# Output projection halves together, second norm one slot earlier, head scales between two expert products

## The chip, the cores and the metric

The kernel runs on one core of one Trainium2 chip. The metric is the device time of one execution in microseconds, the median of several runs. It is a single program written out for each engine: PE (TensorE), ACT (ScalarE), DVE (VectorE), POOL (GpSimd) and SP (SyncE), which issues the DMAs.

## What is computed

A transformer layer on tokens of shape 16 x 256 x 128 in fp32: 16 sequences of 256 tokens, width 128. All inputs beside the tokens are weights.

```python
x = L0_attn_tokens
x = x + attn(layernorm(x))       # 16 heads, keys of 16, values of 64
x = x + moe(layernorm(x))        # 16 experts of width 64, top 4, and a shared expert

# attn: q, k, v l2-normed per head
sim = einsum('bhid,bhjd->bhij', q, k)
aggr = einsum('bhij,bhjd->bhid', square(relu(sim)), v)
out = tanh_norm(aggr) * tanh(silu(gates))      # tanh_norm scales each head's row
return out @ Wout

# moe: scores = sigmoid(x @ gate_kernel) + bias; 2 best of 4 groups, then 4 best experts
y = sum over the experts of combine * (silu(x @ w_gate) * (x @ w_up)) @ w_down
return y + (silu(x @ sw_gate) * (x @ sw_up)) @ sw_down
```

## The kernel before

**Steps and stages.** The kernel works on one sequence of 256 tokens at a time and overlaps seven stages of different sequences. `step(s)` runs for s = -2 to 18. In step s the attention proper (A) is done for sequence s, the first norm and the q/k and v products (L) for s + 2, the gate products and norms of values (P, N) for s + 1, the attention output and the second norm (O) for s - 1, the experts (F) for s - 2 and the expert output (D) for s - 3. `OFFSET` holds these distances. In steps 2 to 13 every stage runs.

**Slots.** A step has eight slots, one for each pair of heads. `FILL` (lines 44 to 54) is an order written out by hand: for each slot the jobs that PE does between the attention products. In a slot PE does the jobs of `FILL[k]`, then the scores of pair k + 1 (line 467), then the values product of pair k (line 499). The values product waits for POOL, which squares the relus (line 326, two multiplies of 128 x 512 in each slot). The relus themselves are ACT's (line 601, two in each slot, ahead of all else that ACT does in it).

**The jobs that matter here.** `qk` and `v`: products of the normed tokens (lines 358 to 360, three matmuls of a high and low split each). `gu` 0 to 8: gate and up products of a pair of experts, the last that of the shared expert. `rT` and `cT`: transposes of the head scales and of the routing weights (line 411). `rB` and `cB` 0 to 3: their spreading over the partitions (line 417). `y` 0 and 1: the two token halves of the attention output projection (line 421), which wait until all four `rB` are read. `x2T`: transposes of the second norm's rows (line 426), `lg`: router logits (line 430), `y2` 0 and 1: the expert output (line 440), which waits until all four `cB` are read.

**Banks.** The fillers share four PSUM banks. The job with number n in `ORDER` (the fill order run together, skips included) has bank n modulo 4, and `wait_for_bank` makes it wait until the job four places before it has been read (the `read` semaphores); where that one is a skip or does not run, the next four before. `evacuate` (ACT) follows the same fill order: it copies `xT`, `qk`, `v`, `x2T`, `rT`, `cT` out of PSUM and does the silu of `gu`. DVE's reads are written by hand in its own `step`.

**The other engines around the change.** DVE's list has for each slot: `gated_heads` (line 901, needs ACT's square of the pair, line 610), `gate_up` (line 855: up times silu, frees the bank of `gu`), `scale_heads` and `scale_hidden` (lines 863 and 872, free `rB` and `cB`), `low_parts` (line 737, frees `qk`), `sums` (line 744, from ACT's squares of `v`), `residual_row` (line 911, frees `y`), `row_stats` (lines 670 to 675), `normed_rows` (line 679, releases `x2T`). `head_scales` waits for ACT's tanh of the norms (line 618, behind the silu of product 4) and then has four short instructions on 128 x 32 elements, each waiting for the one before or queued behind it: lines 783, 788, 789 and 790; the last releases `rT`. POOL has in each slot the two multiplies of line 326, in slots 4 to 7 also one of the values' scaling (line 344), in slot 1 the root of the first norm, in slot 6 that of the second (`root`, line 317). The root waits for `row_stats`. SP's list has the load of the residual rows (waits for `y`), the load of the tokens, the store of the q/k rows (waits for both `low_parts`) and their loads in another layout.

Of the kernel before, what the change touches and what calls it, by code (L numbers as in the profile page):

```python
# [12 lines left out]
P = 128  # L13
# [8 lines left out]
def bass_attn_moe_layer_kernel(nc, tokens, Wqg, Wkv, Wout, gate_kernel, gate_bias,  # L22
# [20 lines left out]
    SKIP = ("-", "skip", 0)  # L43
# [8 lines left out]
        [("L", "qk", 1), ("L", "v", 0), ("F", "cB", 1), ("L", "v", 1), SKIP],  # L52
        [("L", "v", 2), ("F", "cB", 2), ("L", "v", 3), ("F", "cB", 3), ("O", "x2T", 0), SKIP],
    ]
    ORDER = [job for slot in FILL for job in slot]
    assert len(FILL) == SLOTS and len(ORDER) % 4 == 0
# [8 lines left out]
    FIRST_STEP, LAST_STEP = -2, B + 2  # L65

    with ExitStack() as ctx:
# [213 lines left out]
        def _(pool):  # L281
# [37 lines left out]
            def step(s, q, on, at):  # L319
                for k in range(SLOTS):  # L320
                    if "A" in on:
                        for h in (2 * k, 2 * k + 1):

                            wait(pool, values_done, 8 * s + (h - 4) // 2 + 1)
                            pool.wait_ge(relu_done, 16 * s + h + 1)
                            pool.tensor_tensor(p[h % 4][:], r[h % 2][:], r[h % 2][:], ALU.mult).then_inc(probs_done, 1)  # L326
                    if k == 1 and "L" in on:
                        pool.wait_ge(ch_l, 3 * (s + 3))
                        root(rstd1, var1, rstd1_ready)
                    if k == 1 and at == FIRST_STEP:  # L330
                        tables()
                    if k == 6 and "O" in on:
                        pool.wait_ge(ch_n, 3 * s)
                        root(rstd2, var2, rstd2_ready)
                    if "P" in on:
                        b = s + 1
                        if k in (4, 5, 6, 7):

                            t, half = divmod(k - 4, 2)
                            pool.wait_ge(vs_ready, b + 1)  # L340
                            pool.wait_ge(read["v"], 4 * b + k - 3)
                            view = v[b % 3][:, t, half * 512:(half + 1) * 512].rearrange("p (h d) -> p h d", d=DV)
                            scale = vs[:, t, half * NP:(half + 1) * NP]
                            pool.tensor_tensor(view, view, broadcast(scale, [P, NP, DV], 2), ALU.mult)\  # L344
                                .then_inc(v_normed, 1)

            run_flat(step)

# [283 lines left out]
        def _(dve):  # L633
# [209 lines left out]
            def step(s, q, on, at):  # L843
# [70 lines left out]
                for k in range(SLOTS):  # L914
# [23 lines left out]
                    if k == 2:  # L938
# [5 lines left out]
                            gate_up([2])  # L944
                        gated_heads(k)
                        if F:
                            gate_up([3, 4])
                    if k == 3:
                        if O:
                            head_scales(link_o, b)  # L950
                            link_o.end()
                        gated_heads(k)
                        if F:
                            gate_up([5])
# [27 lines left out]
                    if k == 5:  # L982
# [4 lines left out]
                        if O:  # L987
                            dve.wait_ge(x_back[pq], (b - pq) * 8 + 16)
                            residual_row(0)
                        if L_on:  # L990
                            low_parts(0, s + 2)
                        if O:
                            residual_row(1)
                            dve.wait_ge(read["y"], 2 * b + 2)
                            row_stats(link_n, x1[pq], st2, mv2, var2)
                            link_n.end()
                        if F:
                            scale_hidden([0])
                    if k == 6:
                        gated_heads(k)  # L1000
                        if L_on:
                            low_parts(1, s + 2)
                        if at == FIRST_STEP:
                            value_weights()
                        if L_on:
                            sums(0, s + 2)
                        if F:
                            scale_hidden([1])
                        if O:
                            wait(dve, done["lg"], b)  # L1010
                            dve.wait_ge(rstd2_ready, b + 1)
                            normed_rows(x1[pq], mv2, rstd2, xn2, ln2_ready)
                        if L_on:
                            sums(1, s + 2)
                    if k == 7:
                        gated_heads(k)
                        if L_on:
                            sums(2, s + 2)
                        if F:
                            scale_hidden([2])  # L1020
                        if L_on:
                            sums(3, s + 2)
                        if F:
                            scale_hidden([3])
                        if O:
                            dve.wait_ge(x2h_ready, b + 1)
                            dve.tensor_tensor(x2l[:], bank[("x2T", 0)][:, 0:N], x2h[:].bitcast(F32), ALU.subtract)\
                               .then_inc(read["x2T"], 1)

            run_flat(step)  # L1030

# [20 lines left out]
```

## Time and profile before

| what | value |
|---|---|
| median of 3 runs | 753.18 us (752.52 to 755.59) |
| the profiled execution | 755.62 us |
| its span, first to last instruction | 753.6 us |
| PE busy | 680.0 us, 90% of the span |
| PE weight loads | 525.0 us, 70% |
| DVE busy | 543.5 us, 72% |
| ACT busy | 431.8 us, 57% |
| POOL busy | 354.3 us, 47% |
| mean granted clock of TensorE | 0.971 |
| chain that ended last | PE 48%, DVE 29%, ACT 12%, issue 9% |

The profile is that of one execution. Its busy times are sums over the whole span, with a start in which the stages fill up and an end in which they run dry. In a timeline each row is a group of equal instructions: its start, how long from the first's start to the last's end, engine, line, operation, what it writes and reads, how many; in brackets the idle time of that engine before it and what ended it. The granted clock is given as a share of full speed.

### The profile page before, as it was taken

What the parts mean: (1) busy time and instruction counts of PE and PEld (TensorE: products, weight loads), DVE (VectorE), ACT (ScalarE), POOL (GpSimd) and SP (SyncE); (2) the same over time, 40 slices, a digit from 0 to 9 for tenths busy, and PEclk for the clock granted to TensorE, in tenths of its full rate; (3) what the DMA queues carried; (4) which work ended last, traced back from release to release, by engine and by line L of the source; (5) the groups of instructions that cost most, each with busy time, mean ns of one, the idle gap of its engine ahead of it and who ended that gap; (6) DMA issues with size and microseconds to landing.
All of it is one profiled execution on the core that took longest, in us unless ns stands there. A gap on an engine that the chain in (4) does not pass through costs nothing.

```text
span 753.6 us, 15281 instructions
## 1 busy us (share of the span) xinstructions
PE 680.0 (90%) x5160; PEld 525.0 (70%) x5160; DVE 543.5 (72%) x1739; ACT 431.8 (57%) x986; POOL 354.3 (47%) x368
## 2 busy tenths in 40 slices
PE   3676898999999999999999999999999999998876
PEld 2544476777777777777777777777777777666775
DVE  4555558687887968687877968686878868686653
ACT  4575666656665675656666675756566656453211
POOL 3245565554646464554555463645546464643000
PEclk9887999999999999999999999999999999999789
DMA  9994949394654829191845739190927548000000
GB/s 265 112 142 58 137 57 127 39 139 52 119 72 93 97 69 113 31 141 29 131 59 106 85 79 106 64 117 18 152 33 118 66 91 92 2 15 2 8 7 8
DMA packets 72829, 61.24 MB, mean 81 GB/s; under 512 B 8624, under 2 KB 72496, under 8 KB 72752
## 3 DMA queue, kind: packets, MB, share of 16 engines
q1 hardware_dynamic: 72752, 60.26, 54.8%
q8 instruction: 42, 0.69, 0.4%
q14 instruction: 35, 0.29, 0.1%
HBM read 41.37 MB, written 18.87 MB: 80 GB/s over the span
## 4 chain that ended last, share of the span: by engine, by line
PE 48%; DVE 29%; ACT 12%; issue 9%; DMA 1%; POOL 1%; DVEq 0%; SPq 0%; ACTq 0%; POOLq 0%
PE ps_f L440 9%; PE ps_f L421 8%; PE ps_a L499 7%; PE ps_f L358 6%; PE ps_f L360 4%; PE ps_f L359 4%; DVE it L855 4%; DVE norms_y L663 3%; ACT sq L565 3%; DVE norms_t L662 3%; PE ps_s L467 3%; PE ps_f L400 3%; ACT v L562 2%; ACT r L601 2%; DVE it L872 2%
## 5 line engine op out<-in xcount | busy, mean ns | idle before, releaser
L326 POOL TENSOR_TENSOR p<-r 128x512 f32<-128x512 f32 x256 | 263.8, 1051 | 316.0 <-ACT r L601 283.2
L601 ACT ACTIVATE r<-ps_s 128x512 f32<-128x512 f32 x256 | 141.8, 618 | 84.0 <-PE ps_s L467 79.7
L499 PE MATMUL ps_a<-p,v 128*64 128x256 f32 x1024 | 146.2, 397 | 3.0 <-DVE big L901 1.6
L499 PEld LDWEIGHTS ps_a<-p,v 128*64 128x64 f32 x1024 | 64.5, 137 | 43.3 <-POOL p L326 4.8
L593 ACT ACTIVATE it<-ps_f 128x256 f32<-128x256 f32 x144 | 55.5, 385 | 64.4 <-PE ps_f L360 61.3
L901 DVE TENSOR_TENSOR big<-ps_a,wt 128x256 f32<-128x256 f32 x128 | 53.6, 420 | 39.6 <-ACT big L610 38.5
L855 DVE TENSOR_TENSOR it<-ps_f,it 128x256 f32<-128x256 f32 x144 | 58.9, 419 | 29.4 <-ACT it L593 28.8
L440 PE MATMUL ps_f<-wdown,it 128*128 128x128 f32 x576 | 71.3, 285 | 3.3 <-DVE it L872 3.3
L440 PEld LDWEIGHTS ps_f<-wdown,it 128*128 128x128 f32 x576 | 68.7, 199 | 4.3 <-DVE it L872 4.3
L467 PE MATMUL ps_s<-qkt 64*128 64x256 f32 x512 | 66.0, 333 | 3.4 <-ACT r L601 1.9
L344 POOL TENSOR_TENSOR v<-v,vs 128x512 f32<-128x512 f32 x64 | 66.6, 1042 | 3.4 <-DVE vs L778 3.4
L610 ACT ACTIVATE big<-ps_a 128x256 f32<-128x256 f32 x128 | 53.3, 416 | 25.9 <-PE ps_f L400 23.4
L421 PEld LDWEIGHTS ps_f<-wout,big 128*128 128x128 f32 x512 | 61.5, 197 | 5.8 <-issue 5.8
L421 PE MATMUL ps_f<-wout,big 128*128 128x128 f32 x512 | 65.3, 283 | 0.0
L467 PEld LDWEIGHTS ps_s<-qkt 64*128 64x128 f32 x512 | 39.1, 186 | 26.6 <-issue 11.4
L744 DVE TENSOR_REDUCE norms_m<-sq 128x8 f32<-128x512 f32 x64 | 43.7, 683 | 19.1 <-ACT sq L565 19.1
L571 ACT ACTIVATE wt<-ps_f 128x512 f32<-128x512 f32 x64 | 38.4, 600 | 29.4 <-PE ps_f L360 28.9
L737 DVE TENSOR_TENSOR qk_parts<-ps_f,qk_parts 128x512 fp32r<-128x512 f32 x32 | 22.1, 691 | 42.5 <-ACT qk_sq L557 42.5
L358 PE MATMUL ps_f<-x2h,weg_hi 128*128 128x256 f32 x144 | 48.6, 337 | 4.0 <-DVE it L855 2.6
L562 ACT ACTIVATE v<-ps_f 128x512 f32<-128x512 f32 x64 | 41.9, 654 | 6.6 <-PE ps_f L360 4.0
L863 DVE TENSOR_TENSOR big<-ps_f,big 128x512 f32<-128x512 f32 x64 | 42.2, 684 | 4.7 <-PE ps_f L417 4.5
L872 DVE TENSOR_TENSOR it<-ps_f,it 128x512 f32<-128x512 f32 x64 | 43.3, 684 | 2.2 <-PE ps_f L417 1.5
(153 smaller groups left out, 1524.5 us busy)
## 6 DMA issues: line engine op xcount, KB each, us to landing
qk_rows<-qk_parts SPq DMA_DIRECT2D x16, 1024.0 KB, 4.7
qkt<-qk_rows SPq DMA_DIRECT2D x64, 256.0 KB, 10.0
qkt<-qk_rows SPq DMA_DIRECT2D x128, 128.0 KB, 9.4
x_in<-in_L_attn_tokens SPq DMA_DIRECT2D x16, 128.0 KB, 2.2
x_res<-in_L_attn_tokens SPq DMA_DIRECT2D x16, 128.0 KB, 14.3
out<-o_sb SPq DMA_DIRECT2D x16, 128.0 KB, 13.4
big<-in_L_attn_Wqg SPq DMA_DIRECT2D x1, 640.0 KB, 4.1
big<-in_L_attn_Wkv SPq DMA_DIRECT2D x1, 640.0 KB, 5.4
```

The costliest lines, as they stand in the source:

```text
L326: pool.tensor_tensor(p[h % 4][:], r[h % 2][:], r[h % 2][:], ALU.mult).then_inc(probs_done, 1)
L344: pool.tensor_tensor(view, view, broadcast(scale, [P, NP, DV], 2), ALU.mult)\
L358: pe.matmul(dst, stat[0], mov[0], start=True, stop=False)
L421: last = pe.matmul(ps[:, 0:D], aw[pb][:, c, tok[j]], wout[:, c, :], start=(c == 0), stop=(c == NP - 1))
L440: last = pe.matmul(ps[:, 0:D], it[:, c, tok[j]], wdown[:, c, :], start=(c == 0), stop=(c == FC - 1))
L467: last = pe.matmul(ps_s[e][:, t * N:(t + 1) * N], qkt[q][rows, 1, k, t * P:(t + 1) * P], qkt[q][rows, 0, k, :], start=True, stop=True)
L499: last = pe.matmul(ps_a[k % 2][64 * e:64 * e + 64, 0:N], v[s % 3][:, t, h * DV:(h + 1) * DV], p[h % 4][:, t * N:(t + 1) * N], start=(t == ...
L562: act.activation(v[b % 3][:, j // 2, (j % 2) * 512:(j % 2 + 1) * 512], ps[:], ACT.Copy)
L593: act.activation(it[:, j, :], ps[:, 0:N], ACT.Silu).then_inc(silu_done, 1)
L601: act.activation(r[h % 2][:], ps_s[h % 2][:], ACT.Relu).then_inc(relu_done, 1)
L855: dve.tensor_tensor(it[:, c, :], bank[("gu", c)][:, N:2 * N], it[:, c, :], ALU.mult)\
L872: dve.tensor_tensor(part, bank[("cB", j)][:].rearrange("p (c n) -> p c n", n=N), part, ALU.mult).then_inc(read["cB"], 1)
```

## The change

In the fill order `rT` goes ahead of `gu` 6, `y` 1 ahead of `qk` 0, `cB` 1 ahead of `v` 0, `x2T` from the end of slot 7 to between `v` 0 and `v` 1 in slot 6, `cB` 2 and `cB` 3 ahead of `v` 2 and `v` 3, and a skip takes the free place in slot 7. POOL takes the second norm's root behind its last work of slot 5 instead of ahead of its values' scaling in slot 6. DVE has `head_scales` between `gate_up` 3 and 4, both residual rows and the statistics ahead of the first `low_parts`, `normed_rows` directly behind `gated_heads` in slot 6, the low part of `x2T` in slot 6 between `sums` 0 and 1, and in slots 6 and 7 the hidden scales each ahead of the sums. With the order the banks move too: `rT` is now the job four places behind `gu` 4, `gu` 6 that behind `g` 2, `x2T` that behind `cB` 0, `v` 1 that behind `qk` 1, `lg` that behind `cB` 3.

```diff
--- before.py
+++ after.py
@@ -45,12 +45,12 @@
         [("F", "lg", 0), ("D", "y2", 0), ("D", "y2", 1)],
         [("N", "ones", 0), ("F", "gu", 0), ("P", "g", 0), ("N", "nT", 0), ("F", "gu", 1)],
         [("F", "gu", 2), ("P", "g", 1), ("F", "gu", 3), ("F", "gu", 4)],
-        [("P", "g", 2), ("F", "gu", 5), ("F", "cT", 0), ("F", "gu", 6), ("O", "rT", 0)],
+        [("P", "g", 2), ("F", "gu", 5), ("F", "cT", 0), ("O", "rT", 0), ("F", "gu", 6)],
         [("O", "rB", 0), ("O", "rB", 1), ("F", "gu", 7), ("O", "rB", 2), ("L", "xT", 0), ("O", "rB", 3), ("P", "g", 3),
          ("F", "gu", 8)],
-        [("O", "y", 0), ("L", "qk", 0), ("O", "y", 1), ("F", "cB", 0)],
-        [("L", "qk", 1), ("L", "v", 0), ("F", "cB", 1), ("L", "v", 1), SKIP],
-        [("L", "v", 2), ("F", "cB", 2), ("L", "v", 3), ("F", "cB", 3), ("O", "x2T", 0), SKIP],
+        [("O", "y", 0), ("O", "y", 1), ("L", "qk", 0), ("F", "cB", 0)],
+        [("L", "qk", 1), ("F", "cB", 1), ("L", "v", 0), ("O", "x2T", 0), ("L", "v", 1)],
+        [("F", "cB", 2), ("L", "v", 2), ("F", "cB", 3), ("L", "v", 3), SKIP, SKIP],
     ]
     ORDER = [job for slot in FILL for job in slot]
     assert len(FILL) == SLOTS and len(ORDER) % 4 == 0
@@ -329,9 +329,6 @@
                         root(rstd1, var1, rstd1_ready)
                     if k == 1 and at == FIRST_STEP:
                         tables()
-                    if k == 6 and "O" in on:
-                        pool.wait_ge(ch_n, 3 * s)
-                        root(rstd2, var2, rstd2_ready)
                     if "P" in on:
                         b = s + 1
                         if k in (4, 5, 6, 7):
@@ -343,6 +340,9 @@
                             scale = vs[:, t, half * NP:(half + 1) * NP]
                             pool.tensor_tensor(view, view, broadcast(scale, [P, NP, DV], 2), ALU.mult)\
                                 .then_inc(v_normed, 1)
+                    if k == 5 and "O" in on:
+                        pool.wait_ge(ch_n, 3 * s)
+                        root(rstd2, var2, rstd2_ready)
 
             run_flat(step)
 
@@ -944,11 +944,13 @@
                             gate_up([2])
                         gated_heads(k)
                         if F:
-                            gate_up([3, 4])
-                    if k == 3:
+                            gate_up([3])
                         if O:
                             head_scales(link_o, b)
                             link_o.end()
+                        if F:
+                            gate_up([4])
+                    if k == 3:
                         gated_heads(k)
                         if F:
                             gate_up([5])
@@ -987,45 +989,44 @@
                         if O:
                             dve.wait_ge(x_back[pq], (b - pq) * 8 + 16)
                             residual_row(0)
-                        if L_on:
-                            low_parts(0, s + 2)
-                        if O:
                             residual_row(1)
                             dve.wait_ge(read["y"], 2 * b + 2)
                             row_stats(link_n, x1[pq], st2, mv2, var2)
                             link_n.end()
+                        if L_on:
+                            low_parts(0, s + 2)
                         if F:
                             scale_hidden([0])
                     if k == 6:
                         gated_heads(k)
-                        if L_on:
-                            low_parts(1, s + 2)
-                        if at == FIRST_STEP:
-                            value_weights()
-                        if L_on:
-                            sums(0, s + 2)
-                        if F:
-                            scale_hidden([1])
                         if O:
                             wait(dve, done["lg"], b)
                             dve.wait_ge(rstd2_ready, b + 1)
                             normed_rows(x1[pq], mv2, rstd2, xn2, ln2_ready)
                         if L_on:
-                            sums(1, s + 2)
-                    if k == 7:
-                        gated_heads(k)
+                            low_parts(1, s + 2)
+                        if at == FIRST_STEP:
+                            value_weights()
+                        if F:
+                            scale_hidden([1])
                         if L_on:
-                            sums(2, s + 2)
-                        if F:
-                            scale_hidden([2])
-                        if L_on:
-                            sums(3, s + 2)
-                        if F:
-                            scale_hidden([3])
+                            sums(0, s + 2)
                         if O:
                             dve.wait_ge(x2h_ready, b + 1)
                             dve.tensor_tensor(x2l[:], bank[("x2T", 0)][:, 0:N], x2h[:].bitcast(F32), ALU.subtract)\
                                .then_inc(read["x2T"], 1)
+                        if L_on:
+                            sums(1, s + 2)
+                    if k == 7:
+                        gated_heads(k)
+                        if F:
+                            scale_hidden([2])
+                        if L_on:
+                            sums(2, s + 2)
+                        if F:
+                            scale_hidden([3])
+                        if L_on:
+                            sums(3, s + 2)
 
             run_flat(step)
```

## Rows read from the trace of the kernel before

The timelines begin in slot 5 of step 8, at 392.86 us, and go on into step 9; those of rows 6 are from step 14.

**Rows 1.** Sums by stretch: us, busy us of each engine, granted clock, DMA share, GB/s.

```profile
180.00:640.00 460.00, 443.86 (x3540) 347.35 (x3539) 360.84 (x1158) 289.25 (x671) 238.35 (x242) 1.00 0.59 85
...
700.00:754.00 54.00, 39.02 (x247) 35.71 (x245) 26.27 (x98) 8.80 (x25) 0.69 (x1) 0.84 0.02 6
```

**Rows 2.** Waits, longest first: us in total, times, longest us.

```profile
PE ps_f L411 <- DVE rs L790: 9.9, 14, 0.8
```

**Rows 3.** Timeline of PE, steps 8 and 9: start us, us, instructions, idle before.

```profile
392.86 2.05 PE L421 MATMUL ps_f<-wout,big 128*128 128x128 f32 x16
...
395.46 1.95 PE L421 MATMUL ps_f<-wout,big 128*128 128x128 f32 x16
...
397.17 0.48 PE L417 MATMUL ps_f<-ct,sel 128*128 128x256 f32 x2
...
399.02 0.39 PE L358 MATMUL ps_f<-xh,wqk_hi 128*128 128x256 f32 x1
...
400.53 0.40 PE L417 MATMUL ps_f<-ct,sel 128*128 128x256 f32 x2
...
400.77 0.39 PE L358 MATMUL ps_f<-wv_hi,xh 128*128 128x512 f32 x1
...
405.44 0.44 PE L426 MATMUL ps_f<-ident,xn 128*128 128x128 f32 x2 [0.32 <-ACT sq L565]
...
408.04 4.26 PE L440 MATMUL ps_f<-wdown,it 128*128 128x128 f32 x36 [0.16 <-DVE it L872]
...
425.55 0.38 PE L411 MATMUL ps_f<-ident,cs 128*32 128x128 f32 x2
...
427.36 0.38 PE L411 MATMUL ps_f<-ident,rs 128*32 128x128 f32 x2 [0.70 <-DVE rs L790]
...
427.67 0.50 PE L467 MATMUL ps_s<-qkt 64*128 64x256 f32 x4
...
434.73 2.05 PE L421 MATMUL ps_f<-wout,big 128*128 128x128 f32 x16
```

**Rows 4.** Timeline of POOL: slot 6 of step 8, slot 2 of step 9, slot 7 of step 14.

```profile
398.91 2.04 POOL L326 TENSOR_TENSOR p<-r 128x512 f32<-128x512 f32 x2 [2.83 <-ACT r L601]
...
424.82 2.04 POOL L326 TENSOR_TENSOR p<-r 128x512 f32<-128x512 f32 x2 [3.50 <-ACT r L601]
...
653.08 2.04 POOL L326 TENSOR_TENSOR p<-r 128x512 f32<-128x512 f32 x2
```

**Rows 5.** Timeline of DVE, slots 1 to 3 of step 9.

```profile
418.40 0.42 DVE L855 TENSOR_TENSOR it<-ps_f,it 128x256 f32<-128x256 f32 x1 [0.87 <-ACT it L593]
...
424.23 0.75 DVE L855 TENSOR_TENSOR it<-ps_f,it 128x256 f32<-128x256 f32 x2
...
424.89 1.03 DVE L783 TENSOR_TENSOR nn<-nn,bound 128x32 f32<-128x32 f32 x1
...
425.95 0.95 DVE L788 CAST split_hi<-nn 128x32 fp32r<-128x32 f32 x1
...
426.94 0.18 DVE L789 COPY rs<-split_hi 128x32 f32<-128x32 f32 x1
```

**Rows 6.** Timeline of DVE, slot 7 of step 14.

```profile
652.22 1.98 DVE L679 TENSOR_SCALAR xn<-x,mv,rstd 128x128 f32<-128x128 f32 x2 [1.11 <-POOL rstd L317]
```

**Rows 7.** Timeline of DVE, slots 5 and 6 of step 8.

```profile
399.57 0.42 DVE L901 TENSOR_TENSOR big<-ps_a,wt 128x256 f32<-128x256 f32 x1
...
401.22 0.69 DVE L737 TENSOR_TENSOR qk_parts<-ps_f,qk_parts 128x512 fp32r<-128x512 f32 x1 [1.23 <-ACT qk_sq L557]
...
403.40 0.59 DVE L679 TENSOR_SCALAR xn<-x,mv,rstd 128x128 f32<-128x128 f32 x2
```

**Rows 8.** Timeline of ACT, slots 5 and 6 of step 8.

```profile
395.72 0.60 ACT L555 ACTIVATE qk_parts<-ps_f 128x512 fp32r<-128x512 f32 x1 [2.06 <-PE ps_f L360]
...
398.17 1.09 ACT L601 ACTIVATE r<-ps_s 128x512 f32<-128x512 f32 x2 [0.85 <-PE ps_s L467]
...
399.14 0.39 ACT L610 ACTIVATE big<-ps_a 128x256 f32<-128x256 f32 x1
```

## The prediction

> **What bounds the kernel now.** I read the sums by stretch first. Between 180 and 640 us TensorE (PE) is busy for 443.86 of 460 us, at a granted clock of 1.00; DVE has 360.84, POOL 238.35 [rows 1]. So over the twelve steps in which every stage runs the time is PE's own work plus PE's waits, and a delay on another engine counts only where PE comes to wait for it. Next the waits: the largest that repeats is PE at the transpose of the head scales (line 411), 9.9 us in 14 times, released by DVE's line 790 [rows 2]. Last the timeline of one step, which says where in it the waits lie. The reader is to see three [rows 3]: 0.32 us at the transpose of the second norm (x2T, line 426), 0.16 us at the expert output (y2, line 440) and 0.70 us at the transpose of the head scales (rT, line 411). The step repeats after 434.73 - 392.86 = 41.87 us. At most 0.32 + 0.16 + 0.70 = 1.18 us of a step is there to be won by a reordering, since no PE instruction is added or removed. The question is what the new order makes PE wait for.
>
> Three rules of this kernel carry the working. PE, ACT, DVE and POOL each run their list in order. A PSUM bank goes from a job to the fourth job after it in the fill order, and the later one waits until the earlier has been read. And DVE's small operations that stay in SBUF are held up while POOL multiplies: line 783 starts at 424.89, 0.07 us after POOL's line 326, and takes 1.03 us; line 788 starts at 425.95, inside POOL's second multiply, and takes 0.95; the copy of line 789 comes after both and takes 0.18 [rows 4, 5]. Two operations in a row are each held: line 679 takes 1.98 us for two where POOL is busy [rows 4, 6], 0.59 where it is mostly free [rows 7]. Reads of PSUM (lines 855, 901, 737) keep their 0.4 to 0.7 us.
>
> **Part 1: both halves of the output projection in a row (slot 5).** PE's work is the same, so slot 6 still begins at 399.02 [rows 3]. But the q/k product behind them starts later by one half, 397.17 - 395.46 = 1.71 us. ACT's copy of it moves from 395.72 to about 397.45, and behind it ACT has the copy, the square and a gate tanh before the next two relus. From 395.72 to 398.17 less the idle 0.85 us that is 1.6 us, of which 0.1 overlaps the next instruction: the relus start at 398.95 instead of 398.17, and the slack of 0.85 us is gone. The square of the attention pair moves by the same 0.78, from 399.14 to 399.9 [rows 8], DVE's multiply behind it (line 901) from 399.57 to 400.3 [rows 7], and POOL's two multiplies of that slot from 398.91 to 399.65, until 401.7 [rows 4]. SP's store of the q/k rows waits for DVE's second line 737, which comes some 0.5 us later, and its loads behind it; the scores that need them come a step later, so half a us of a 41.87 us step costs nothing; without that cover it would cost the same 0.5.
>
> **Part 2: the second norm earlier (root in slot 5, transpose in slot 6).** The second half of the output ends where it did less one q/k product, so the statistics are ready by about 398; POOL's next multiply is only released at 399.65, so the root between them costs nothing. If the statistics came late, two multiplies would be queued behind the root, and PE's values product waits for those. In DVE's list the normed rows now stand right behind line 901 of slot 6, so they start at 400.3 + 0.35 = 400.65. That is at the border of POOL's two multiplies (399.65 to 400.7 to 401.7): the first row gets through, the second is held until the second multiply ends, as in [rows 6], so they are done at about 401.8 instead of 400.65 + 0.59 = 401.25. PE reaches the transpose after q/k 1, its new neighbour cB1 and v0, that is at 399.02 + 1.51 + 0.24 = 400.77, plus some 0.1 for the change of type [rows 3]. With 0.15 us from DVE's end to PE's start (line 789 ends at 427.12, line 790 some 0.1 later, PE starts at 427.36 [rows 3, 5]) it stands until about 401.95: **a stall of 1.1 us**. Behind it v1 has the bank of q/k 1, which DVE frees with line 737 (0.69 us), queued behind the normed rows: free at about 402.5, while the transpose is through at 402.3: another 0.2. The transpose itself (0.37 to 0.45 us) moves from slot 7 to slot 6. So slot 6 ends later by 1.1 + 0.2 + 0.45, about 1.8 us.
>
> Slot 7 gives back the transpose (0.37) and its old wait (0.32), and the expert output's wait of 0.16 goes, since the hidden scales now lie before v3. But the router logits (lg) now take the bank of the last hidden-scale product cB3. DVE reads that only after the sums and the earlier scale, which are late with ACT's squares: about 408.6 where PE arrives at 408.4: 0.25 us. In sum 1.8 - 0.69 - 0.16 + 0.25 = **+1.2 us a step** at the start of the expert output. DVE's routing chain behind it shifts as a whole; POOL's blocks shift with it, and DVE idles 0.87 us before the norm chain of slot 2 [rows 5], which takes up what else is late.
>
> **Part 3: head scales between products 3 and 4, and rT ahead of product 6 (slots 2, 3).** The tanh that the head scales wait for stands on ACT ahead of the relus, so it is ready. DVE's two products of 424.23 are 0.33 us apart, so line 783 would start at 424.56 instead of 424.89 and take some 0.19; line 788 at 424.79. POOL's multiplies start at 424.82 [rows 4, 5]. Whichever of the two wins, line 789 at 425.02 and line 790 behind it are held, the one until the first multiply ends (425.9), the other until the second does (426.9). Only then comes product 4 (0.34 to 0.42 us): 427.25. And rT, now one place earlier, has product 4's bank: it starts at about 427.35, where it starts already (427.36) [rows 3]. But before, product 6 lay in front of it and filled part of the wait; now product 6 comes after. From the hidden-scale transpose at 425.55 over product 6 to rT's arrival at 426.66 is 1.11 us; the same two jobs now lie between rT and the scores, which took 427.67 - 427.36 = 0.31 before. **+0.8 us a step**, and rT's stall grows from 0.70 to about 1.55. The earlier rT would help rB0, which waits for nothing in these steps. Unknown here is the copy of line 789: no row has it beside a POOL multiply. If it is never held, lines 789 and 790 are through at 425.9, product 4 at 426.3, rT starts at 426.4 and the slot ends 0.15 us earlier than before. 
>
> **Sum.** Twelve full steps at 1.2 + 0.8 = 2.0 us: 24. The first step with attention output has no experts: about 1.2. The two steps without new q/k and v work have less of PE's own work ahead of the transpose, and their normed rows were held by POOL before too [rows 6]: I take 0.9 each for slots 5 to 0, between 0 and 1.5, and 0.8 for slot 3, together 3.4. In the last step with attention output the logits must wait for both of DVE's last hidden scales (0.69 us each, like line 737 [rows 7]): about 1.4. Together 30 us. The profiled execution took 755.62 us, so it would become about 786; it lies 2.4 above the median of the runs, 753.18, to which I add the same 30: **783 us**.
>
> **Rivals.**
> (a) *Only one of the two delays is real.* If the copy of line 789 is not held, 15 steps at 1.2 and -0.15 give about +17: 770. If instead the second normed row slips between POOL's multiplies and ACT catches up, slot 3 alone gives 12 to 15 times 0.8: about 765. For it: both rest on starts that lie within 0.1 us of POOL's. Against: those starts hang on one another, not on chance; the step repeats to 0.01 us. Chance 0.24.
> (b) *Faster.* The waits of [rows 3] go and nothing replaces them: rT's scales would be ready before POOL's multiplies, the normed rows before PE arrives. 1.18 us in 13 steps: -15, so 738. It decides at the normed rows: they would have to be done by 400.6, 1.2 us before my figure, and product 4 by 425.7. For it: the plain reading, that a producer made earlier and a consumer made later ends a wait. Against: ACT's list behind q/k 0, and POOL's multiplies. Chance 0.10.
> (c) *Nothing to measure*: gains and losses cancel, for instance the slot 3 term at -0.15 with half the slot 6 stall. Within 0.5%, about what a measurement of this kernel can tell from no change: 753. Chance 0.06.
> (d) *The clock falls.* After 700 us, where PE is busy for 39.02 of 54 us, its granted clock is 0.84 [rows 1], between its levels of 2.4 and 1.2 GHz. Two stalls of 1.1 and 1.55 us a step could do that in the middle too. At 0.9 over the steady part, 444 us of PE work grow by about 50 us: 830. Against: with waits of 0.7 us each step the clock stays at 1.00. Chance 0.03.
> My forecast has 0.57.
>
> **Range and chances.** The forecast's own bounds: 1.5 to 2.5 us a step, 776 to 790. The range takes in (a) down to 764 and reaches to 794, for the upper bound of +1.1 in slot 3; what is left out is (b), (c) and (d), 0.19. Slower 0.57 + 0.24 + 0.03 = 0.84, within 0.5% 0.06, faster 0.10.
>
> **What would show it.** In the profile after: PE waits at line 426 for line 679, about 1.1 us each step, at line 411 about 1.5 us for line 855 (no longer 790); lines 789 and 790 take about 0.9 us each; relus of slot 6 start 0.7 us later after slot 5 begins; the step takes about 43.9 us. A step below 41.87 us, or line 679 at 0.59 for two with no wait behind it, would make the forecast wrong.

## The result, and the profile after

The change makes the kernel slower: 804.57 us median (798.93 to 804.8), before 753.28 us in the same runs, ratio 1.066 (95% interval 1.061 to 1.071). The forecast was slower by 30 us; it is 51. The profiled execution spans 797.0 us, 43.4 more than before, and is the fastest of those taken: its mean granted clock is 0.946, the four executions of 804.5 to 806 us have 0.934 to 0.938. One execution of `no_part3` below, 810.2 us, counts as slow by its length and is left out of that run's ratio.

The sums by stretch come first, as before (columns as in [rows 1]; us, busy us of PE, its weight loads, DVE, ACT and POOL, then granted clock, DMA share, GB/s):

```profile
97.00:180.00 83.00, 73.81 (x535) 53.72 (x535) 55.70 (x184) 48.34 (x109) 41.71 (x43) 0.94 0.57 80
180.00:640.00 460.00, 429.11 (x3342) 329.01 (x3341) 346.40 (x1097) 276.03 (x636) 225.83 (x229) 0.98 0.56 80
640.00:740.00 100.00, 88.73 (x660) 66.97 (x660) 67.27 (x206) 47.13 (x111) 46.33 (x47) 0.93 0.26 38
```

In the steady stretch PE was busy for 443.86 of 460 us at a clock of 1.00; now it is for 429.11, and the clock is 0.98. Two things have gone wrong, then: PE stands more, and for part of the time it runs slower. PE's waits name the place where it stands (us in total, times, longest us):

```profile
PE ps_f L426 <- DVE xn L679: 34.1, 16, 2.6
...
PE ps_f L411 <- DVE it L855: 10.3, 16, 2.0
```

34.1 us in 16 times at line 426 are the transposes of the second norm, x2T. At line 411 PE now waits for product 4 (line 855) instead of line 790 [rows 2]. The timeline of PE through one full step (from slot 5 of step 4 to slot 5 of step 5) is to be laid beside [rows 3]:

```profile
239.62 3.84 PE L421 MATMUL ps_f<-wout,big 128*128 128x128 f32 x32
...
245.78 0.39 PE L358 MATMUL ps_f<-xh,wqk_hi 128*128 128x256 f32 x1
...
249.77 0.41 PE L426 MATMUL ps_f<-ident,xn 128*128 128x128 f32 x2 [2.09 <-DVE xn L679]
250.27 0.50 PE L358 MATMUL ps_f<-wv_hi,xh 128*128 128x512 f32 x1
...
252.62 0.51 PE L417 MATMUL ps_f<-ct,sel 128*128 128x256 f32 x2
...
256.33 0.62 PE L430 MATMUL ps_f<-wroute,xn 128*128 128x16 f32 x4
256.79 4.26 PE L440 MATMUL ps_f<-wdown,it 128*128 128x128 f32 x36
...
274.33 0.38 PE L411 MATMUL ps_f<-ident,cs 128*32 128x128 f32 x2
275.15 0.39 PE L411 MATMUL ps_f<-ident,rs 128*32 128x128 f32 x2 [0.44 <-DVE it L855]
...
276.18 0.51 PE L467 MATMUL ps_s<-qkt 64*128 64x256 f32 x4
...
283.25 0.94 PE L421 MATMUL ps_f<-wout,big 128*128 128x128 f32 x6
```

This step takes 283.25 - 239.62 = 43.63 us where it took 41.87. Slot 7 of the old step, which [rows 3] does not show, began here:

```profile
403.00 0.50 PE L358 MATMUL ps_f<-wv_hi,xh 128*128 128x512 f32 x1
```

The two steps stretch by stretch:

| stretch | before | after | difference | forecast |
|---|---|---|---|---|
| slot 5, from the output halves to slot 6 | 6.16 | 6.16 | 0 | 0 |
| slot 6 | 3.98 | 6.84 | +2.86 | +1.8 |
| slot 7, to the expert output | 5.04 | 4.17 | -0.87 | -0.6 |
| to the transpose of the routing weights | 17.51 | 17.54 | +0.03 | 0 |
| from there to the next scores | 2.12 | 1.85 | -0.27 | +0.8 |
| the rest | 7.06 | 7.07 | +0.01 | 0 |
| sum | 41.87 | 43.63 | +1.76 | +2.0 |

So the sum of a step was nearly right, out of two terms that were both wrong. What is missing is in other steps: the first two, and from then on every other one. The step behind the one shown takes 45.13 us, and around its x2T PE does this (sums by stretch again, then the timeline of PE there):

```profile
288.00:291.00 3.00, 3.00 (x24) 2.17 (x23) 1.89 (x7) 3.00 (x7) 1.55 (x2) 1.00 0.00 0
291.00:294.00 3.00, 0.81 (x5) 0.29 (x3) 3.00 (x5) 1.80 (x5) 2.17 (x3) 0.98 0.00 0
294.00:297.00 3.00, 3.00 (x11) 1.76 (x13) 1.67 (x4) 1.97 (x5) 0.00 (x0) 0.50 0.75 254
297.00:300.00 3.00, 3.00 (x18) 1.95 (x16) 1.42 (x3) 2.05 (x6) 2.69 (x3) 0.95 0.48 148
```

```profile
293.40 0.41 PE L426 MATMUL ps_f<-ident,xn 128*128 128x128 f32 x2 [2.09 <-DVE xn L679]
293.91 0.79 PE L358 MATMUL ps_f<-wv_hi,xh 128*128 128x512 f32 x1
294.50 0.63 PE L359 MATMUL ps_f<-wv_lo,xh 128*128 128x512 f32 x1
```

PE stands for 2.09 us, and then its granted clock is 0.50, that is 1.2 instead of 2.4 GHz: the matmul of line 359 takes 0.63 us, 0.39 to 0.40 at the full clock. Such a dip costs 45.13 - 43.63 = 1.50 us. In the profiled execution seven of the twelve full steps (slot 5 of step 2 to slot 5 of step 14) have one, though the wait at x2T is 2.09 us in all twelve; the executions of 804.5 us have a lower mean clock.

The whole 43.4 us of this execution: 1.9 before the first output projection; 5.9 in the step after it (39.35 to 45.22); 31.6 in the twelve full steps (149.35 to 683.38 is 534.03, before 502.48), of which 12 times 1.76 is 21.1 and the clock 10.5; 4.1 behind them.

Why the rows are late is in the timelines of DVE and POOL beside the x2T of the step shown first (beside [rows 4, 7]):

```profile
246.06 0.68 DVE L872 TENSOR_TENSOR it<-ps_f,it 128x512 f32<-128x512 f32 x1
247.15 0.42 DVE L901 TENSOR_TENSOR big<-ps_a,wt 128x256 f32<-128x256 f32 x1 [0.41 <-ACT big L610]
247.49 2.13 DVE L679 TENSOR_SCALAR xn<-x,mv,rstd 128x128 f32<-128x128 f32 x2
249.54 0.68 DVE L737 TENSOR_TENSOR qk_parts<-ps_f,qk_parts 128x512 fp32r<-128x512 f32 x1
```

```profile
244.87 0.69 POOL L317 TENSOR_TENSOR rstd<-var,minus_half 128x2 f32<-128x2 f32 x1 [2.02 <-DVE var L675]
246.50 2.04 POOL L326 TENSOR_TENSOR p<-r 128x512 f32<-128x512 f32 x2 [0.94 <-ACT r L601]
248.50 1.04 POOL L341 TENSOR_TENSOR v<-v,vs 128x512 f32<-128x512 f32 x1
```

The normed rows start at 247.49, as forecast behind line 901 (7.87 us into slot 5; the forecast 400.65 is 7.79 into it). Free of POOL they need 0.59 us [rows 7]. They take 2.13, one by one 1.13 and 1.08: the first row lies beside POOL's second multiply, which starts at about 247.50 (each of the two takes 1.04 us), and the second beside the scaling of the values (line 341 now, line 344 before). Both were held, by one instruction of POOL each.

### The profile page after: what moved, and what is told of

Read it like the earlier page. It is cut to its first block, busy times and chain, and to the rows that moved or that the text cites. A ratio compares the mean times of both kernels' runs of the same rounds, so it can differ in the third digit from the quotient of the medians.

```text
span 797.0 us, 15294 instructions
## 1 busy us (share of the span) xinstructions
PE 699.2 (88%) x5160; PEld 530.1 (67%) x5160; DVE 549.3 (69%) x1739; ACT 434.9 (55%) x986; POOL 354.2 (44%) x368
## 4 chain that ended last, share of the span: by engine, by line
PE 55%; DVE 22%; issue 12%; ACT 9%; POOL 1%; DMA 1%; DVEq 0%; SPq 0%; POOLq 0%; ACTq 0%
PE ps_a L499 10%; PE ps_f L440 8%; PE ps_f L358 7%; PE ps_f L421 7%; PE ps_f L360 5%; PE ps_f L359 5%; PE ps_s L467 4%; DVE xn L679 4%; DVE norms_y L663 3%; PE ps_f L400 3%; DVE norms_t L662 3%; PE ps_f L417 2%; DVE it L855 2%; ACT r L601 2%; DVE norms_t L661 2%
## 5 line engine op out<-in xcount | busy, mean ns | idle before, releaser
L601 ACT ACTIVATE r<-ps_s 128x512 f32<-128x512 f32 x256 | 139.4, 601 | 70.5 <-PE ps_s L467 65.4
L499 PE MATMUL ps_a<-p,v 128*64 128x256 f32 x1024 | 153.5, 414 | 2.8 <-DVE big L901 1.9
L499 PEld LDWEIGHTS ps_a<-p,v 128*64 128x64 f32 x1024 | 68.4, 144 | 45.5 <-issue 6.9
L467 PE MATMUL ps_s<-qkt 64*128 64x256 f32 x512 | 68.7, 344 | 5.9 <-ACT r L601 3.3
L610 ACT ACTIVATE big<-ps_a 128x256 f32<-128x256 f32 x128 | 51.0, 398 | 31.6 <-PE ps_f L400 23.4
L421 PEld LDWEIGHTS ps_f<-wout,big 128*128 128x128 f32 x512 | 58.4, 192 | 5.8 <-issue 5.8
L421 PE MATMUL ps_f<-wout,big 128*128 128x128 f32 x512 | 61.3, 278 | 0.0
L317 POOL TENSOR_TENSOR rstd<-var,minus_half 128x2 f32<-128x2 f32 x32 | 22.1, 690 | 73.4 <-DVE var L675 68.1
L562 ACT ACTIVATE v<-ps_f 128x512 f32<-128x512 f32 x64 | 39.1, 611 | 24.5 <-PE ps_f L360 22.1
L555 ACT ACTIVATE qk_parts<-ps_f 128x512 fp32r<-128x512 f32 x32 | 19.6, 612 | 55.9 <-PE ps_f L360 55.9
```

The source lines that it names most:

```text
L421: last = pe.matmul(ps[:, 0:D], aw[pb][:, c, tok[j]], wout[:, c, :], start=(c == 0), stop=(c == NP - 1))
L467: last = pe.matmul(ps_s[e][:, t * N:(t + 1) * N], qkt[q][rows, 1, k, t * P:(t + 1) * P], qkt[q][rows, 0, k, :], start=True, stop=True)
L499: last = pe.matmul(ps_a[k % 2][64 * e:64 * e + 64, 0:N], v[s % 3][:, t, h * DV:(h + 1) * DV], p[h % 4][:, t * N:(t + 1) * N], start=(t == ...
L601: act.activation(r[h % 2][:], ps_s[h % 2][:], ACT.Relu).then_inc(relu_done, 1)
L610: act.activation(a2[:, pair, :], ps_a[pair % 2][:, 0:N], ACT.Square).then_inc(a2_done, 1)
```

## The experiments

**First, the change taken apart: without its third part, and the third part alone.**

```diff
 # no_part3, against the changed kernel
-        [..., ("F", "cT", 0), ("O", "rT", 0), ("F", "gu", 6)],
+        [..., ("F", "cT", 0), ("F", "gu", 6), ("O", "rT", 0)],
-  gate_up([3]); head_scales(link_o, b); gate_up([4])        # slot 2
+  gate_up([3, 4])                                          # slot 2
+  head_scales(link_o, b)                                   # slot 3, first
```

`part3_only` makes the opposite edit in the kernel before.

> The change without its third part: head scales and rT stand as before. Theory (the loss is the stall at x2T in slot 6 and the clock that falls with it; part 3 is worth about -0.15 us a step): a step takes 43.6 + 0.15 to 0.3 us where the clock stays up, rT's wait is back at 0.70 us, x2T's stays 2.09 us, the median stays at 800 to 808 us. Rival (part 3 carries a good share of the loss, 0.8 us a step as in the prediction): 790 us or less.

> The kernel before with the third part alone: head scales between products 3 and 4, rT ahead of product 6. Theory: line 790 slips in front of POOL's second multiply, rT starts about 0.95 us earlier, the step falls from 41.87 to about 41.7 us, the time is 750 to 752 us. Rival of the prediction (0.8 us a step more): 764 us.

Without its third part the kernel takes 803.39 us median (794.99 to 810.2), ratio 1.061 (1.052 to 1.070): 1 us less than the changed kernel, within the spread, so the third part is not the loss. Its full steps without a dip take 43.89 us, 0.26 more, and rT waits 0.70 us again. Its dips differ in length: six of the twelve steps have one, and they cost from 1.3 us to 2.8 (a step of 46.66). The third part alone takes 753.47 us, ratio 0.9995 (0.9979 to 1.0011), no change, and a little above the 750 to 752 expected. Its full steps fell from 41.87 to 41.65 us, which over twelve is 2.6 us; in the profiled execution the start took it back (the first output projection at 104.63 instead of 102.26 us), why is not shown. The forecast of +0.8 us a step falls. The timelines of the changed kernel show why (beside [rows 5] and [rows 4]):

```profile
273.32 0.18 DVE L783 TENSOR_TENSOR nn<-nn,bound 128x32 f32<-128x32 f32 x1
273.53 0.18 DVE L788 CAST split_hi<-nn 128x32 fp32r<-128x32 f32 x1
273.75 0.92 DVE L789 COPY rs<-split_hi 128x32 f32<-128x32 f32 x1
274.58 0.18 DVE L790 TENSOR_TENSOR rs<-nn,split_hi 128x32 f32<-128x32 f32 x1
274.68 0.41 DVE L855 TENSOR_TENSOR it<-ps_f,it 128x256 f32<-128x256 f32 x1
```

```profile
273.59 2.08 POOL L326 TENSOR_TENSOR p<-r 128x512 f32<-128x512 f32 x2 [3.50 <-ACT r L601]
```

Line 789, the copy, is held for 0.92 us, as forecast. But line 790, queued behind it with no wait of its own, starts at 274.58 and takes its plain 0.18: it got in at the border between POOL's two multiplies. The second of them starts at 274.59 and takes 1.08 us instead of 1.04.

**Second, does the clock fall because PE stands?** The same order and the same waits, but PE has something to do meanwhile. The eight added products (each recorded as two) write to unused columns and nothing reads them; everything else is computed as before.

```diff
 # stall_filled, against the changed kernel
                 elif kind == "x2T":
+                    for _ in range(8):
+                        pe.matmul(ps_a[0][:, N:N + P], ident[:], ident[:], start=True, stop=True)
                     pe.wait_ge(ln2_ready, b + 1)
```

> The changed kernel with 8 matmuls of 128 columns more ahead of the wait for the second norm's rows, into a part of a PSUM bank that nothing reads; they take about 1.7 us of the 2.09 us in which PE stands there. Their results are not used. Theory (the clock falls because PE stands still there): no step shows a lower clock, every full step takes about 43.6 us, the stall row shows 0.4 us, the time falls to about 785 us though PE does more. Rival (the clock falls for another reason, or the stall is not what it follows): steps of 45.1 us stay, 800 us or more.

785.23 us median (781.37 to 788.3), ratio 1.041 (1.036 to 1.045): with more work the kernel is 19 us faster. PE at x2T, and the sums by stretch:

```profile
241.67 1.95 PE L425 MATMUL ps_a<-ident 128*128 128x128 f32 x16
243.83 0.44 PE L428 MATMUL ps_f<-ident,xn 128*128 128x128 f32 x2 [0.21 <-DVE xn L681]
```

```profile
97.00:180.00 83.00, 78.82 (x600) 58.76 (x600) 60.28 (x197) 50.28 (x116) 43.01 (x44) 0.98 0.62 86
180.00:640.00 460.00, 446.95 (x3554) 349.91 (x3553) 350.53 (x1102) 280.26 (x646) 230.22 (x233) 1.00 0.54 80
```

The transpose starts 10.07 us into the step, where it started 10.15 into it; 0.21 us of standing are left, every full step takes 43.60 to 43.69 us, and the clock of the steady stretch is 1.00 again. So some 19 of the 51 us are the clock, the other 32 the later order itself. Between the two profiled executions (797.0 and 781.4 us) it is 15.6: 10.5 in the full steps, 3.9 in the step ahead of them, 2.2 behind them, less 1.0 at the start.

**Third, what holds the normed rows?** Two edits from opposite sides. `norm_early` takes them ahead of POOL's multiplies; `pool_waits` makes POOL wait for them.

```diff
 # norm_early, against the changed kernel: DVE, slot 5
+                        if O:
+                            wait(dve, done["lg"], b)
+                            dve.wait_ge(rstd2_ready, b + 1)
+                            normed_rows(x1[pq], mv2, rstd2, xn2, ln2_ready)
                         if F:
                             scale_hidden([0])
 # and the same four lines taken out of slot 6
```

```diff
 # pool_waits, against the changed kernel: POOL
+                        if k == 6 and "O" in on:
+                            pool.wait_ge(ln2_ready, s)
                         for h in (2 * k, 2 * k + 1):
```

> The changed kernel with DVE's normed rows ahead of the first hidden scale in slot 5, so before POOL's two multiplies of slot 6. Theory (POOL holds line 679): the pair takes 0.6 us instead of 2.1, PE no longer waits for it at x2T, and v1 then waits about 1.0 us for line 737, which is late with ACT's copy of q/k 1; a step takes about 42.5 us at full clock, 760 to 768 us. Rival (the rows are late with the output projection, not through POOL): the stall at x2T stays over 1.5 us and the time over 790 us.

> The changed kernel, but POOL's two multiplies of slot 6 wait until the second norm's rows are written, so POOL idles about 1.5 us there in every step and holds nobody. Theory (line 679 is held by POOL): the pair takes 0.6 us instead of 2.1, x2T's wait falls from 2.09 to about 0.6 us, v1 waits about 0.5 us more for line 737, values of slot 6 may wait for POOL by up to 0.5 us; a step takes 42.3 to 43.0 us at full clock, 762 to 775 us, faster although one engine was made to wait. Rival (the rows are late for another reason): the wait at x2T stays near 2 us and the time at 800 us or above.

`norm_early`: 769.59 us median, 1.6 above the 760 to 768 expected, ratio 1.020 (1.018 to 1.022), 42.23 us a step, no dip of the clock in the full steps. DVE's rows and PE's next wait:

```profile
235.95 0.59 DVE L679 TENSOR_SCALAR xn<-x,mv,rstd 128x128 f32<-128x128 f32 x2
...
238.01 0.69 DVE L737 TENSOR_TENSOR qk_parts<-ps_f,qk_parts 128x512 fp32r<-128x512 f32 x1 [0.54 <-ACT qk_sq L557]
```

```profile
237.41 0.38 PE L426 MATMUL ps_f<-ident,xn 128*128 128x128 f32 x2
238.76 0.50 PE L358 MATMUL ps_f<-wv_hi,xh 128*128 128x512 f32 x1 [0.97 <-DVE qk_parts L737]
```

The pair takes 0.59 us and nobody waits for it; now v1 waits 0.97 us for its bank, late with ACT's copy and square of q/k 1. That wait lay hidden behind the other. Of the 14.2 us by which this profiled execution is longer than the kernel before only 4.4 lie in the full steps; 6.4 lie behind them, where x2T waits 2.7 us for a hidden scale.

`pool_waits`: 766.03 us median, ratio 1.016 (1.014 to 1.018), about 42.3 us a step (229.65 to 271.95). Here are POOL, DVE and PE of one step:

```profile
238.20 2.04 POOL L328 TENSOR_TENSOR p<-r 128x512 f32<-128x512 f32 x2 [2.60 <-DVE xn L681]
```

```profile
237.53 0.59 DVE L681 TENSOR_SCALAR xn<-x,mv,rstd 128x128 f32<-128x128 f32 x2
```

```profile
238.27 0.41 PE L428 MATMUL ps_f<-ident,xn 128*128 128x128 f32 x2 [0.56 <-DVE xn L681]
```

DVE's pair takes 0.59 us where it took 2.13, though it starts at the same place in the step (7.88 us into slot 5), and the wait at x2T falls from 2.09 to 0.56. One added wait on POOL makes the kernel 38 us faster than the changed one. That POOL's instructions hold the rows is shown by both: the rows need 0.59 us where POOL runs nothing when each of them starts, whether they or POOL were moved.

**Fourth, the first part alone.** In the kernel before, `y` 1 goes ahead of `qk` 0 and both residual rows with the statistics ahead of the first low part; x2T stays at the end of slot 7.

```diff
 # halves_only, against the kernel before
-        [("O", "y", 0), ("L", "qk", 0), ("O", "y", 1), ("F", "cB", 0)],
+        [("O", "y", 0), ("O", "y", 1), ("L", "qk", 0), ("F", "cB", 0)],
```

> The kernel before with its first part alone: both output halves in a row and both residual rows ahead of the first low part; x2T stays at the end of slot 7. Theory (the late ACT copy of q/k 0 harms only what reads it soon, and x2T in slot 7 is out of its reach): ACT's relus of slot 6 start 0.7 us later, but PE's waits change by under 0.3 us a step, no step with a low clock, 750 to 757 us. Rival (the delay of ACT's list is itself the loss): over 0.8 us a step, 764 us or more.

756.99 us median, ratio 1.0034 (1.0017 to 1.0052); a step takes 42.03 us, 0.16 more. ACT is late as forecast, and of this 0.13 us show at x2T:

```profile
195.70 0.44 PE L426 MATMUL ps_f<-ident,xn 128*128 128x128 f32 x2 [0.45 <-ACT sq L565]
```

It was 0.32 [rows 3]. The first part by itself costs little. In the changed kernel, where x2T reads DVE's results in slot 6, the same late lists come to bear; how much of its loss goes to them alone no run separates.

**Fifth, the idea of part 3 one place earlier.** The head scales ahead of product 3, so that all four instructions are through before POOL's multiply.

```diff
 # heads_before_3, against the kernel before; with rT ahead of gu 6 as in the change
+                        if O:
+                            head_scales(link_o, b)
+                            link_o.end()
                         if F:
                             gate_up([3, 4])
```

> The kernel before with rT ahead of product 6 and the head scales ahead of product 3 instead of behind it. Theory (their four instructions then end before POOL's multiply of that slot begins, so none is held): lines 783 to 790 take 0.2 us each, product 4 is read by the time PE arrives, rT's wait of 0.70 us is gone, the step falls to 41.1 to 41.3 us, the time to 741 to 748 us. Rival (something behind, such as rB0, takes the wait over): 41.6 us or more, 750 us or more.

745.71 us median (742.3 to 747.33), ratio 0.989 (0.988 to 0.991): 1.1% faster than the kernel before, as expected (741 to 748). A step takes 41.10 us.

```profile
251.20 0.18 DVE L783 TENSOR_TENSOR nn<-nn,bound 128x32 f32<-128x32 f32 x1
251.41 0.18 DVE L788 CAST split_hi<-nn 128x32 fp32r<-128x32 f32 x1
251.63 0.18 DVE L789 COPY rs<-split_hi 128x32 f32<-128x32 f32 x1
251.72 0.18 DVE L790 TENSOR_TENSOR rs<-nn,split_hi 128x32 f32<-128x32 f32 x1
```

```profile
252.53 0.38 PE L411 MATMUL ps_f<-ident,cs 128*32 128x128 f32 x2
252.75 0.38 PE L411 MATMUL ps_f<-ident,rs 128*32 128x128 f32 x2
```

Four instructions in 0.70 us, where they took 2.3 before (424.89 to 427.2, [rows 5]); POOL's first multiply starts at 251.80, 0.08 us after the last of them has started, and rT no longer waits.

**Sixth, two attempts at more.** `combo`: the halves together, normed rows ahead of the first hidden scale, x2T as first job of slot 7, head scales ahead of product 3. `best`: `heads_before_3` with the skip ahead of x2T (so that it has the bank of cB2) and the last two hidden scales ahead of their sums.

```diff
 # combo, against the changed kernel, beside the edits of norm_early and heads_before_3
-        [("L", "qk", 1), ("F", "cB", 1), ("L", "v", 0), ("O", "x2T", 0), ("L", "v", 1)],
-        [("F", "cB", 2), ("L", "v", 2), ("F", "cB", 3), ("L", "v", 3), SKIP, SKIP],
+        [("L", "qk", 1), ("F", "cB", 1), ("L", "v", 0), ("L", "v", 1), SKIP],
+        [("O", "x2T", 0), ("F", "cB", 2), ("L", "v", 2), ("F", "cB", 3), ("L", "v", 3), SKIP],
 # best, against heads_before_3
-        [("L", "v", 2), ("F", "cB", 2), ("L", "v", 3), ("F", "cB", 3), ("O", "x2T", 0), SKIP],
+        [("L", "v", 2), ("F", "cB", 2), ("L", "v", 3), ("F", "cB", 3), SKIP, ("O", "x2T", 0)],
```

> A version meant to beat both: halves in a row; head scales ahead of product 3 with rT ahead of product 6; normed rows ahead of the first hidden scale in slot 5; x2T as the first job of slot 7, behind v1 of slot 6. Theory: normed rows are done before POOL's multiplies, PE waits for them nowhere, v1 has the bank of cB0, rT's wait is gone: of the 1.18 us of waits in a step at most 0.3 stays, 40.8 to 41.2 us a step, 737 to 745 us. Rival (a new bank wait in slot 7, v3 behind x2T's low part or logits behind v2, takes their place): 41.6 us a step or more, 750 us or more.

> The kernel before with rT ahead of product 6 and the head scales ahead of product 3, and two small moves in slot 7: the skip goes ahead of x2T, so that x2T has the bank of cB2 instead of v2, and DVE takes hidden scales 2 and 3 each ahead of the sums. Theory (each wait in a step is a bank or a list order, and goes when its producer comes first): x2T's wait of 0.32 us and the expert output's of 0.17 go, the step falls from 41.10 us to 40.6 to 40.8, the time to 735 to 742 us. Rival (ACT's squares or the last scale take the wait over): 41.0 us a step, 743 us or more.

Both missed. `combo`: 758.78 us, ratio 1.006 (1.004 to 1.008), 41.87 us a step. The rival held: in every full step v3 waits 1.39 us (and the clock of the steady stretch is 1.00) for the bank of x2T, which DVE frees with x2T's low part, in this version behind hidden scale 2 in slot 7.

```profile
241.12 0.50 PE L358 MATMUL ps_f<-wv_hi,xh 128*128 128x512 f32 x1 [1.39 <-DVE x2l L1020]
```

`best`: 749.08 us median, but from 744.68 to 755.21, ratio 0.995 (0.992 to 0.998). Its full steps are the shortest, 40.92 us, and it is still slower than `heads_before_3`. The two steps behind them, without new q/k and v work, pay: x2T waits there 1.92 us where it waited 1.08, and the clock falls; they take 79.8 us together, in `heads_before_3` 70.2. Here are the sums from 640 to 700 us of `best`, then of `heads_before_3`:

```profile
640.00:700.00 60.00, 52.10 (x358) 40.65 (x358) 36.54 (x130) 19.36 (x48) 19.91 (x20) 0.86 0.03 8
```

```profile
640.00:700.00 60.00, 50.45 (x394) 39.19 (x394) 43.45 (x153) 21.99 (x56) 19.87 (x20) 0.97 0.03 8
```

## Why the prediction was right or wrong

Forecast was 30 us, measured 51, above the range of 764 to 794. Three terms failed: the clock, put at nothing (19 us of the medians), the hold on the normed rows (12 times 1.06 us too little) and part 3 (12 times 1.07 us too much). The last two cancel, so what is left over is about the clock.

**Right: the direction, and why.** PE's own work sets the time, PE's waits decide; x2T moved to where its rows are not ready, and the list of ACT behind q/k 0 and POOL's instructions are the reason. Slot 5 keeps its length (6.16 us), the root costs nothing (done at 245.56, the multiplies start at 246.50), the normed rows start within 0.1 us of the forecast.

**Wrong: "the clock stays", the main error.** The prediction gave its rival (d) a chance of 0.03, on the ground that with waits of 0.7 us each step the clock had stayed at 1.00, and added nothing for it. It is 19 of the 51 us (`stall_filled` 785.23 against 804.57). In size the rival was too large: it took 0.9 for the steady stretch, and it was 0.98. The ground did not carry: a wait of 0.7 us says nothing of one of 2. This error hangs on the next: with one wait of 0.97 us a step (`norm_early`) or 1.39 (`combo`) the clock of the steady stretch stayed at 1.00; of the waits in full steps only the one of 2.09 brought it down. Whether the stalls that were forecast, 1.1 and 1.55 us in the same step, would have moved it no run shows.

**Wrong: the hold on the normed rows.** "The first row gets through, the second is held until the second multiply ends": both were held, one instruction of POOL further. The stall is 2.09 us where 1.1 was forecast, and slot 6 +2.86 instead of +1.8. The precedent that the prediction names, the rows of step 14 [rows 6], already showed this: one by one they took 0.98 and 1.08 us, the first beside POOL's scaling of the values (652.08 to 653.12), the second (from 653.12) beside the multiply behind it (from 653.08). The step rested on starts within 0.1 us of each other, the prediction knew that of its rival (a) and looked only for what would make the loss smaller. One more held instruction, 1.04 us, should have been the upper bound: 12 times 1.04 is 12 us. The 0.2 us at v1 shrank to 0.1 at most: line 737 started 0.08 us ahead of the end of the rows and ran beside the transpose, which ends at 250.18, line 737 at 250.22, and v1 starts at 250.27.

**Wrong in sign: part 3.** "The one until the first multiply ends, the other until the second does": the first half is as forecast (line 789 took 0.92 us), line 790 got in between. Instead of +0.8 us a step it is -0.27 in the changed kernel, -0.22 alone.
**Smaller terms.** Slot 7 gave back 0.87 us instead of 0.6: 0.75 up to its scores, 0.33 between logits and expert output where 0.16 was forecast, less 0.21 by which the router logits start later behind the values product (1.22 us against 1.01), forecast 0.25. That a step came to 1.76 us beside the forecast 2.0 is luck: slot 6 was put 1.06 us too low and slot 3 1.07 too high. The range, 764 to 794, ended where a longer stall and a fallen clock began. The faster rival (b) fails at the normed rows: they would have had to be done 1.2 us earlier, and even with the rows early (`norm_early`) v1 waits for ACT's copy and square. Its other half, rT without a wait, needs another place for the head scales (`heads_before_3`).

## What to carry to other kernels

When a consumer is moved earlier on the bounding engine, replay the lists of the engines that feed it, with the bank that the consumer now takes; a stall that is ended by one thing can hide a second one behind it (0.97 us at v1 in `norm_early`, behind the 2.09 at x2T). Small DVE operations that stay in SBUF belong ahead of POOL's long ones or well behind them: at their border a forecast should carry one POOL instruction either way, and here it was cheaper to let POOL wait. And price a stall of PE by the clock too: 2.09 us of standing cost nothing more in some steps, 1.5 us in others and up to 2.8 in `no_part3`, and a version with shorter full steps can lose by two long stalls elsewhere (`best`).

## What the runs showed of the hardware

- TensorE's clock fell from 2.4 to 1.2 GHz behind a single standstill of 2.09 us in a stretch where PE was otherwise busy, in seven full steps and not in five others with the same wait and the same work; filled with eight unread products, the same wait left the clock at 1.00. One standstill of 0.97 (`norm_early`) or 1.39 us (`combo`) in each step left it there too.
- Two DVE instructions in a row without a wait between them are not held alike: of the pair of line 679 both were held (1.13 and 1.08 us), while of lines 789 and 790 the first took 0.92 us and the second 0.18. By the record the first row and line 790 each start 0.01 us ahead of POOL's second multiply (247.49 and 247.50; 274.58 and 274.59), and one is held and the other is not. What decides at the border of two POOL instructions was not settled.
- An fp32 copy of 128 x 32 elements within SBUF is held by a POOL multiply (0.92 us against 0.18).
